# A state-space mixer and a gated MLP on one core: the first block's queues rearranged, and its first differences, clamps and skip moved between engines

## The chip, the cores and the metric

The kernel runs on one core of one Trainium2 chip. The metric is device time in microseconds (us), lower is better. The engines are PE (TensorE, the matrix engine), DVE (VectorE), ACT (ScalarE), POOL (GpSimd) and SP (SyncE, which issues the DMAs). Each works through its own queue in order and waits on semaphores for the others.

## The reference

Two sequences of 1024 tokens by 512 go through a mixer of the Mamba-2 kind and then a gated MLP, each behind a layer norm and with a residual. The change touches the mixer alone:

```python
x = x + mixer(layernorm(x)); x = x + ffn(layernorm(x))
proj = hidden @ W_in * mup_vector              # 512 -> 2368: z, xBC, dt
xBC  = silu(conv_b + sum(conv_w[:, k] * shift(xBC, k) for k in range(4)))
dt   = softplus(dt + dt_bias); dA = exp(-dt * exp(A_log))
state = state * dA + (dt * x)[..., None] * B   # 64 heads of 16, 128 states, one token after another
y = einsum(state, C) + D * x
g = y * silu(z); g = g * rsqrt(mean(g * g) + EPS) * norm_w
out = g @ W_out
```

## The kernel before, in words

The 1024 tokens are cut into 8 blocks of 128, and each block (both sequences side by side: 256 columns) into two steps of 64 tokens, numbered c = 0 to 15. Matmuls keep fp32 accuracy by splitting each operand into a rounded part (hi, made by ACT) and the rest (lo, made by DVE as raw minus hi), and by three products: hi hi, hi lo, lo hi (L1223 to L1225). The weights are split once, in the opening, in 14 pieces: `weight_hi(n)` on ACT (L624, L627) and `weight_lo(n)` on DVE (L880, L883). Pieces 0 to 9 are those of W_in and belong to the ten projections of a block, "project(j, e)"; pieces 10 to 13 are W_out. The raw pieces land in buffers that are used for something else later (the ring, xpad, sz, the state, rows, skip, sq, res), so whoever first writes such a buffer waits until that piece is split.

For each block: the rows are normalised (statistics on DVE, L890; the power on POOL, L509; L899), transposed by PE (L1209) and split (`norm_hi` L632, `norm_lo` L905). Projection 0 gives dt. ACT takes it out of PSUM in `evacuate(j, 0)` (four ACTIVATEs of L642, an exp behind a table load L646, a copy L649). DVE finishes softplus by a polynomial of 11 steps, `soft` (L911), and a running sum (L928). That sum goes out to DRAM and comes back broadcast in four 256 KB pieces, the ring. Projections 1 to 5 feed the convolution: ACT starts a pair of tiles (`first_taps`), DVE adds the other taps (`conv_taps`, L936, 30 instructions a block), ACT applies silu (L697). Projections 6 to 9 are z.

For each step, in four groups g of 16 heads: `diff` (POOL, L530) subtracts the ring from a token's own sum, `clamp` (ACT, L715) cuts it at zero, `fade` (ACT, L719) takes the exponential, `mix` (DVE, L991) multiplies it with the masked C B product (`mask_cb` L948), and PE multiplies with the inputs in `group(c, g)` (L1295). `make_xpad` (DVE, L977) prepares those inputs from the transposed x, `make_xw` (POOL, L539) the ones for the state, PE's `update(c, h)` (L1306) and DVE's `update_state` (L998 in step 0) carry the state on; `carry` (PE, L1272) reads it in the next step. Then `make_skip` (ACT, L725: D times x), `make_y` (L1006), `gate` (L1012), `gate_hi` (ACT, L732), `gate_lo` (L1017), and PE's projection out.

The order in which an engine does this is written by hand: each engine's part has a `body(i, first, last)` for a block, and a prologue before it for block 0. In `body` the projections of block i+1 stand between the groups of step 1 of block i. The prologue and the branches `if first` are run once.

## Time and profile before

| | us |
|---|---|
| median of 3 runs | 775.62 (775.45 to 776.03) |
| profiled execution, whole | 774.75 |
| its span | 773.0 |
| PE busy in the span | 742.7 (96%) |
| DVE busy | 518.6 (67%) |
| ACT busy | 492.7 (64%) |
| POOL busy | 294.0 (38%) |

The span runs from the first to the last instruction of the core; the whole execution is 1.75 us longer. Times in the rows are us from the span's start. A row of the timeline merges like instructions that stand behind one another (x and a count); "idle before" in brackets is the time in which the engine stood still, with the work that ended it. Busy time of PE says that an instruction was in flight, not that the array ran at its peak.

### The profile page before, as it was taken

How to read it: one execution, taken by the hardware profiler on the slowest of the kernel's cores; microseconds unless marked ns; L12 is line 12 of the kernel's file. 1: busy time of each engine (PE TensorE's matmuls, PEld its weight loads, DVE VectorE, ACT ScalarE, POOL GpSimd, SP SyncE). 2: the span in 40 equal slices, each digit the busy share in tenths (PEclk: the TensorE clock that was granted, in tenths of full speed). 3: DMA queues.
4: the chain of work that ended last, by engine and by line, in shares of the span. 5: the costliest groups of instructions: out<-in, count | busy, mean ns of one | idle time of the engine just before them, and what ended most of it. 6: DMA issues, size and time to landing. Idle time of an engine off the chain costs nothing.

```text
span 773.0 us, 20312 instructions
## 1 busy us (share of the span) xinstructions
PE 742.7 (96%) x8486; PEld 612.8 (79%) x8486; DVE 518.6 (67%) x845; ACT 492.7 (64%) x933; POOL 294.0 (38%) x235
## 2 busy tenths in 40 slices
PE   4887999999999999999999999889999999999998
PEld 4866888788887887887888887678888888888887
DVE  6968976886887797797797698763633532632331
ACT  6989978978978977978888888634312321321330
POOL 2173285366456536627708718540010011002002
PEclk9978999999999999999999999989999999999999
DMA  9823244484475266365376377855113003003002
GB/s 298 236 67 109 55 95 111 96 243 127 83 213 169 80 148 214 99 148 188 93 204 190 83 200 234 230 159 164 55 56 109 0 28 136 0 14 93 3 1 84
DMA packets 42300, 94.97 MB, mean 123 GB/s; under 512 B 9889, under 2 KB 15777, under 8 KB 42017
## 3 DMA queue, kind: packets, MB, share of 16 engines
q1 hardware_dynamic: 42208, 93.67, 42.6%
q8 instruction: 67, 1.10, 0.6%
q14 instruction: 25, 0.20, 0.1%
HBM read 84.73 MB, written 17.57 MB: 132 GB/s over the span
## 4 chain that ended last, share of the span: by engine, by line
PE 61%; DVE 21%; ACT 10%; issue 5%; DMA 2%; SPq 1%; POOL 1%; DVEq 0%; ACTq 0%; POOLq 0%
PE ps_y L1684 10%; PE ps_proj L1671 10%; DVE cx L936 9%; PE ps_out L1671 6%; PE ps_x L1671 6%; PE ps_proj L1223 4%; PE ps_proj L1224 3%; PE ps_proj L1225 3%; PE ps_x L1272 3%; PE ps_y L1295 3%; DVE ring L991 3%; ACT ring L715 2%; PE ps_out L1319 2%; DVE dt_p L911 2%; PE ps_out L1321 2%
## 5 line engine op out<-in xcount | busy, mean ns | idle before, releaser
L530 POOL TENSOR_TENSOR ring<-tokd,ring 128x1024 f32<-128x1024 f32 x64 | 122.5, 1927 | 189.4 <-ACT tokd L710 126.1
L1223 PE MATMUL ps_proj<-xn_hi,win_x_hi 128*128 128x256 f32 x352 | 104.7, 297 | 1.6 <-DVE xn_lo L905 1.6
L1224 PE MATMUL ps_proj<-xn_lo,win_x_hi 128*128 128x256 f32 x352 | 100.2, 285 | 0.0
L1225 PE MATMUL ps_proj<-xn_hi,win_x_lo 128*128 128x256 f32 x352 | 99.9, 284 | 0.0
L936 DVE SCALAR_TENSOR_TENSOR cx<-cin,consts,cx 128x256 f32<-128x256 f32 x240 | 96.4, 484 | 0.0
L1540 POOL TENSOR_TENSOR res<-res,hidden 128x512 f32<-128x512 f32 (+1 forms) x16 | 20.1, 1257 | 166.3 <-DVE hidden L1603 160.7
L1223 PEld LDWEIGHTS ps_proj<-xn_hi,win_x_hi 128*128 128x128 f32 x352 | 67.6, 192 | 14.8 <-issue 11.5
L991 DVE TENSOR_TENSOR ring<-ring,ps_tok 128x1024 f32<-128x1024 f32 x64 | 75.6, 1215 | 4.7 <-ACT ring L719 4.7
L1223 PE MATMUL ps_proj<-xn_hi,win_z_hi 128*128 128x256 f32 x256 | 74.4, 291 | 0.0
L715 ACT ACTIVATE ring<-ring 128x1024 f32<-128x1024 f32 x64 | 66.8, 1060 | 10.2 <-POOL ring L530 10.2
L1224 PE MATMUL ps_proj<-xn_lo,win_z_hi 128*128 128x256 f32 x256 | 72.5, 283 | 0.0
L1225 PE MATMUL ps_proj<-xn_hi,win_z_lo 128*128 128x256 f32 x256 | 72.4, 283 | 0.0
L1225 PEld LDWEIGHTS ps_proj<-xn_hi,win_x_lo 128*128 128x128 f32 x352 | 67.8, 193 | 0.0
L1224 PEld LDWEIGHTS ps_proj<-xn_lo,win_x_hi 128*128 128x128 f32 x352 | 67.8, 192 | 0.0
L719 ACT ACTIVATE ring<-ring 128x1024 f32<-128x1024 f32 x64 | 65.9, 1056 | 0.1
L1684 PE MATMUL ps_y<-wd,h_hi 128*128 128x512 f32 x165 | 65.8, 399 | 0.0
L1684 PE MATMUL ps_y<-wd,h_lo 128*128 128x512 f32 x165 | 65.0, 394 | 0.0
L1295 PEld LDWEIGHTS ps_y<-ring,xpad 64*32 64x32 f32 x4096 | 45.1, 107 | 20.2 <-issue 12.9
L1561 ACT ACTIVATE silu_g<-ps_out,scales 128x512 f32<-128x512 f32 x24 | 16.6, 691 | 68.0 <-PE ps_x L1671 68.0
L1295 PE MATMUL ps_y<-ring,xpad 64*32 64x64 f32 x4096 | 54.1, 228 | 3.6 <-DVE ring L991 3.0
L1563 ACT ACTIVATE h_hi<-hidden 128x512 fp32r<-128x512 f32 x44 | 27.9, 634 | 40.6 <-DVE hidden L1628 40.6
L548 POOL TENSOR_TENSOR state<-state,whole 128x2048 f32<-128x2048 f32 x14 | 53.1, 3790 | 0.0
(186 smaller groups left out, 1889.6 us busy)
## 6 DMA issues: line engine op xcount, KB each, us to landing
ring<-cum_dram SPq DMA_DIRECT2D x128, 256.0 KB, 5.0
xin<-x SPq DMA_DIRECT2D x8, 512.0 KB, 3.9
res<-x SPq DMA_DIRECT2D x32, 128.0 KB, 2.7
x_dram<-res SPq DMA_DIRECT2D x32, 128.0 KB, 3.1
res<-x_dram SPq DMA_DIRECT2D x16, 256.0 KB, 2.7
out<-res SPq DMA_DIRECT2D x15, 256.0 KB, 2.1
x_in_sb<-x_dram SPq DMA_DIRECT2D x3, 1024.0 KB, 5.6
gate_w_copy<-gate_w SPq DMA_DIRECT2D x4, 704.0 KB, 5.9
```

What stands on the lines that cost most here:

```text
L530: pool.tensor_tensor(ring[:, g, :, :], own, ring[:, g, :, :], ALU.subtract).then_inc(diffed, 1)
L548: pool.tensor_tensor(s, s, whole[:, :, j:j + 1].to_broadcast([P, BATCH * HEADS, HEAD]), ALU.mult).then_inc(state_faded, 1)
L715: act.activation(ring[:, g, :, :], ring[:, g, :, :], ACT.Relu).then_inc(clamped, 1)
L719: act.activation(ring[:, g, :, :], ring[:, g, :, :], ACT.Exp, scale=-1.0).then_inc(faded, 1)
L936: dve.scalar_tensor_tensor(cx[:, m, :, :], cin[:, m, :, k:k + Q], col(C_CW + 4 * m + k), cx[:, m, :, :], ALU.mult, ALU.add).then_inc(tap_m ...
L991: dve.tensor_tensor(ring[:, g, :, :], ring[:, g, :, :], ps_cb.unsqueeze(1).to_broadcast([P, GH, Q]), ALU.mult).then_inc(mixed, 1)
L1223: pe.matmul(out, hi[:, k, :], xn_hi[:, k, :], start=(k == 0), stop=False)
L1224: pe.matmul(out, hi[:, k, :], xn_lo[:, k, :], start=False, stop=False)
L1225: made = pe.matmul(out, lo[:, k, :], xn_hi[:, k, :], start=False, stop=(k == KT - 1))
L1295: made = pe.matmul(ps_y[32 * pair:32 * pair + 32, at:at + Q], xpad[half(b), g * GH + h, :], ring[half(b), g, h, :], start=(c == g == n == ...
L1671: made = pe.matmul(out_ps, a, b, start=(k == 0 and x is xn_hi), stop=(k == KT - 1 and x is xn_lo))
L1684: made = pe.matmul(ps_o[t % 2], a, b, start=(m == 0 and h is h_hi), stop=(m == MT - 1 and h is h_lo))
```

## The change

The changed parts all belong to the opening, that is the prologues and block 0; later blocks keep their order.

- The first rows are loaded, measured, scaled and normalised for each of the two sequences on its own. PE transposes an identity 20 times before the first rows and 6 times behind them (`keep_warm`).
- ACT's and DVE's prologues are reordered: `evacuate(0, 0)` stands between `weight_hi(2)` and `weight_hi(3)`, and three `soft` steps stand between `weight_lo(3)` and `weight_lo(4)`.
- In step 0 DVE does `diff` and `clamp` of the groups 0, 1 and 2 (`opening_diff`, `opening_clamp`); group 3 stays with POOL and ACT.
- In step 0 the skip product is one instruction of POOL, `pool_skip`, in place of eight on ACT.
- The pieces 9 to 13 are split later, and in other places; pieces of W_out land in another order of buffers.
- In block 0 PE does `update(0, 1)` and `group(0, 3)` before it transposes the next block's rows, and projection 9 before `turn_tokd`.

```diff
+        landing += [t[:].rearrange("p m t -> p (m t)") for t in (skip, sq)] + [rows[:], xres[:].rearrange("p m t -> p (m t)")]
...
 
         def piece(n):
...
-            sp.dma_start(xin[:], x_by_block[0]).then_inc(x_in, 16)
+            sp.dma_start(xin[:, 0, :], x_by_block[0, :, 0, :]).then_inc(x_first, 16)
+            sp.dma_start(xin[:, 1, :], x_by_block[0, :, 1, :]).then_inc(x_in, 16)
...
-            norm_scale(0)
+            def opening_scale(b):
+                pool.wait_ge(moments_made, b + 1)
+                pool.tensor_tensor(spread[:, b:b + 1], moments[:, b, 1:2], eps[:, b:b + 1], ALU.add).then_inc(eps_added, 1)
+                pool.wait_ge(eps_added, b + 1)
+                pool.tensor_tensor(rstd[:, b:b + 1], spread[:, b:b + 1], minus_half[:, b:b + 1], ALU.pow).then_inc(rstd_made, 1)
+
+            opening_scale(0)
+            opening_scale(1)
             pool.memset(chain[:, 0::Q], 0.0).then_inc(filled, 1)
-            pool.wait_ge(rstd_made, 1)
+            pool.wait_ge(xn_made, 2)
...
+            def pool_skip(c):
+
+                pool.wait_ge(y_made, c)
+                pool.wait_ge(conv_made, CT * (c // STEPS + 1))
+                at = BATCH * (c % STEPS)
+                pool.tensor_tensor(skip[:].rearrange("p m (b t) -> p m b t", b=BATCH), cx[:, 0:ZT, at:at + BATCH, :],
                                    consts[:, C_D:C_D + ZT].unsqueeze(2).unsqueeze(3).to_broadcast([P, ZT, BATCH, Q]),
                                    ALU.mult).then_inc(skip_made, 1)
...
+                    if opening:
+                        pool.wait_ge(diffed, GROUPS - 1)
+                        diff(0, 0, GROUPS - 1)
                     if not (opening or closing):
...
                     if closing:
-                        last_skip()
+                        pool_skip(c)
                     if not closing:
+                        if opening:
+                            pool.wait_ge(xn_made, 4)
                         for g in range(GROUPS):
+                            if opening and g == 1:
+                                pool.wait_ge(lo_made, LANDED_SKIP)
+                                pool_skip(c)
                             if g == GROUPS - 1 and not opening:
                                 rms_scale(c - 1, 1 - j)
                             diff(i + j, 1 - j, g)
...
             pool.wait_ge(filled, 4)
-            pool.wait_ge(tap_made, N_TAPS)
-            for g in range(GROUPS):
-                diff(0, 0, g)
             body(0, True, False)
...
                 c = STEPS * i
                 if not first:
                     evacuate(i, 6)
-                clamp(c, 0)
-                clamp(c, 1)
-                if not first:
+                if first:
+                    keep_tok(c)
+                    fade(c, 0)
+                else:
+                    clamp(c, 0)
+                    clamp(c, 1)
                     square(c - 1)
                     evacuate(i, 7)
-                keep_tok(c)
-                fade(c, 0)
-                clamp(c, 2)
+                    keep_tok(c)
+                    fade(c, 0)
+                    clamp(c, 2)
                 fade(c, 1)
+                if first:
+                    weight_hi(9)
+                    fade(c, 2)
+                    act.wait_ge(clamped, GROUPS - 1)
                 clamp(c, 3)
-                fade(c, 2)
+                if not first:
+                    fade(c, 2)
                 fade(c, 3)
-                if first:
-                    weight_hi(EVENTS)
-                else:
+                if not first:
                     make_skip(i, 0)
                 evacuate(i, 8)
-                keep_tokd(i, 1)
+                if not first:
+                    keep_tokd(i, 1)
                 evacuate(i, 9)
                 if first:
-                    weight_hi(EVENTS + 1)
+                    keep_tokd(i, 1)
+                    weight_hi(EVENTS)
                 if not last:
                     norm_hi(i + 1, 0)
                     norm_hi(i + 1, 1)
                 if first:
-                    for n in range(EVENTS + 2, PIECES):
-                        weight_hi(n)
-                    act.wait_ge(lo_made, LANDED_SKIP)
-                    make_skip(i, 0)
+                    weight_hi(EVENTS + 1)
...
                 clamp(c + 1, 0)
                 clamp(c + 1, 1)
+                if first:
+                    weight_hi(EVENTS + 2)
                 if not last:
                     evacuate(i + 1, 0)
                 gate_hi(c)
+                if first:
+                    weight_hi(EVENTS + 3)
...
             weight_hi(0)
-            weight_hi(1)
             norm_hi(0, 0)
             norm_hi(0, 1)
-            for n in range(2, 6):
-                weight_hi(n)
+            weight_hi(1)
+            weight_hi(2)
             act.wait_ge(zeroed, 7)
             evacuate(0, 0)
+            weight_hi(3)
             evacuate(0, 1)
+            weight_hi(4)
+            weight_hi(5)
+            evacuate(0, 2)
             first_taps(0, CONV_ORDER[0:2])
-            evacuate(0, 2)
+            evacuate(0, 3)
             first_taps(0, CONV_ORDER[2:4])
             weight_hi(6)
+            evacuate(0, 4)
+            first_taps(0, CONV_ORDER[4:6])
             make_run(0)
-            evacuate(0, 3)
-            first_taps(0, CONV_ORDER[4:6])
+            evacuate(0, 5)
+            first_taps(0, CONV_ORDER[6:8])
+            first_taps(0, CONV_ORDER[8:10])
             weight_hi(7)
-            evacuate(0, 4)
-            first_taps(0, CONV_ORDER[6:8])
-            evacuate(0, 5)
-            first_taps(0, CONV_ORDER[8:10])
             keep_tokd(0, 0)
...
-            weight_hi(9)
             body(0, True, False)
...
+            def opening_stats(b):
+                dve.wait_ge(x_in if b else x_first, 16)
+                dve.bn_stats(stats[:, b, :], xin[:, b, :]).then_inc(stats_made, 1)
+                dve.wait_ge(stats_made, b + 1)
+                dve.bn_aggr(moments[:, b, :], stats[:, b, :]).then_inc(moments_made, 1)
+
+            def opening_normalise(b):
+                dve.wait_ge(rstd_made, b + 1)
+                dve.tensor_scalar(xin[:, b, :], xin[:, b, :], moments[:, b, 0:1], rstd[:, b:b + 1],
+                                  ALU.subtract, ALU.mult).then_inc(xn_made, 1)
+
+            def opening_clamp(g):
+                dve.wait_ge(diffed, g + 1)
+                dve.tensor_scalar(ring[:, g, :, :], ring[:, g, :, :], 0.0, None, ALU.max).then_inc(clamped, 1)
+
+            def opening_diff(g):
+
+                dve.wait_ge(ring_in[g], 32)
+                dve.wait_ge(tokd_kept, 1)
+                own = tokd[:, 0, CUM, g * GH:(g + 1) * GH].unsqueeze(2).to_broadcast([P, GH, Q])
+                dve.tensor_tensor(ring[:, g, :, :], own, ring[:, g, :, :], ALU.subtract).then_inc(diffed, 1)
...
                 mask_cb(c)
                 make_xpad(i, 0)
-                if first:
-                    weight_lo(9)
-                else:
+                if not first:
                     make_x1(c - 2)
                 mix(c, 0)
                 if not first:
                     scale_carry(i, 0)
-                for g in range(1, GROUPS):
-                    mix(c, g)
-                if not last:
+                if first:
+                    opening_diff(2)
+                    opening_clamp(2)
+                mix(c, 1)
+                if first:
+                    weight_lo(9)
+                mix(c, 2)
+                if first:
+                    norm_stats(i + 1)
+                mix(c, 3)
+                if first:
+                    update_state(c, 0)
+                    normalise(i + 1)
+                    update_state(c, 1)
+                    weight_lo(EVENTS)
+                elif not last:
                     norm_stats(i + 1)
                     normalise(i + 1)
-                if first:
-                    weight_lo(EVENTS)
                 if last:
                     mlp_stats(0)
-                update_state(c, 0)
+                if not first:
+                    update_state(c, 0)
                 if last:
                     mlp_normalise(0)
                     mlp_normalise(1)
+                if not last:
+                    norm_lo(i + 1, 0)
+                    norm_lo(i + 1, 1)
                 if first:
                     weight_lo(EVENTS + 1)
-                if not last:
-                    norm_lo(i + 1, 0)
-                    norm_lo(i + 1, 1)
-                update_state(c, 1)
-                if first:
-                    for n in range(EVENTS + 2, PIECES):
-                        weight_lo(n)
+                else:
+                    update_state(c, 1)
                 make_y(c)
                 gate(i, 0)
+                if first:
+                    weight_lo(EVENTS + 2)
...
                 gate_lo(c - 1)
+                if first:
+                    weight_lo(EVENTS + 3)
                 for n in range(1, 4):
                     soft(i + 1, n)
...
-            norm_stats(0)
+            opening_stats(0)
+            opening_stats(1)
+            opening_normalise(0)
+            opening_normalise(1)
             weight_lo(0)
-            normalise(0)
-            weight_lo(1)
             norm_lo(0, 0)
             norm_lo(0, 1)
-            for n in range(2, 6):
+            for n in range(1, 4):
                 weight_lo(n)
-            for n in range(1, LOGN):
+            for n in range(1, 4):
+                soft(0, n)
+            weight_lo(4)
+            weight_lo(5)
+            for n in range(4, LOGN):
                 soft(0, n)
             make_dt(0, opening=True)
...
             conv_taps(0, CONV_ORDER[8:10])
+            opening_diff(0)
+            opening_clamp(0)
             weight_lo(8)
+            opening_diff(1)
+            opening_clamp(1)
             dve.wait_ge(zeroed, 8)
             body(0, True, False)
...
+            def keep_warm(n):
+
+
+                for _ in range(n):
+                    pe.transpose(ps_out[:, 0:P], eye[:], eye[:])
...
                 update(c, 0)
-                turn_tokd(i, 1)
                 if first:
                     pe.wait_ge(lo_made, EVENTS)
-                project(i, 9)
+                    project(i, 9)
+                    turn_tokd(i, 1)
+                else:
+                    turn_tokd(i, 1)
+                    project(i, 9)
                 group(c, 2)
+                if first:
+                    update(c, 1)
+                    group(c, 3)
                 if not last:
                     turn_xn(i + 1, 0)
                     turn_xn(i + 1, 1)
                 if not first:
                     sum_squares(c - 1)
-                update(c, 1)
-                group(c, 3)
+                    update(c, 1)
+                    group(c, 3)
...
             pe.wait_ge(filled, 1)
+            keep_warm(20)
             turn_xn(0, 0, True)
             turn_xn(0, 1, True)
+            keep_warm(6)
             for e in range(8):
                 pe.wait_ge(lo_made, e + 1)
                 project(0, e)
```

DVE, from the last taps of block 0's convolution to the last `mix` of step 0. Before (L936 taps, L880 `weight_lo`, L948 mask, L977 xpad, L991 mix):

```order
L936 SCALAR_TENSOR_TENSOR cx<-cin,consts,cx 128x256 x12
L880 TENSOR_TENSOR win_z_lo<-sz,win_z_hi 128x4x256
L948 TENSOR_TENSOR ps_tok<-ps_tok,causal 128x64
L977 TENSOR_TENSOR xpad<-ps_x,tokd 128x32x16 x2
L880 TENSOR_TENSOR win_z_lo<-state,win_z_hi 128x4x256
L991 TENSOR_TENSOR ring<-ring,ps_tok 128x1024 x4
```

and now (L985 taps, L943 `opening_diff`, L936 `opening_clamp`, L997 mask, L1026 xpad, L1042 mix):

```order
L985 SCALAR_TENSOR_TENSOR cx<-cin,consts,cx 128x256 x12
L943 TENSOR_TENSOR ring<-tokd,ring 128x1024
L936 TENSOR_SCALAR ring<-ring 128x1024
L907 TENSOR_TENSOR win_z_lo<-sz,win_z_hi 128x4x256
L943 TENSOR_TENSOR ring<-tokd,ring 128x1024
L936 TENSOR_SCALAR ring<-ring 128x1024
L997 TENSOR_TENSOR ps_tok<-ps_tok,causal 128x64
L1026 TENSOR_TENSOR xpad<-ps_x,tokd 128x32x16 x2
L1042 TENSOR_TENSOR ring<-ring,ps_tok 128x1024
L943 TENSOR_TENSOR ring<-tokd,ring 128x1024
L936 TENSOR_SCALAR ring<-ring 128x1024
L1042 TENSOR_TENSOR ring<-ring,ps_tok 128x1024
```

Three differences and three clamps have come in, `weight_lo(8)` stands behind the first pair and the mask behind the second.

POOL, from the zeroing of xpad on. Before (L530 diff, L539 xw, L507 and L509 the scale of the next rows, L556 the squares):

```order
L522 MEMSET xpad 128x2048
L530 TENSOR_TENSOR ring<-tokd,ring 128x1024 x4
L539 TENSOR_TENSOR xw<-xpad,tokd 128x1024
L507 TENSOR_TENSOR spread<-moments,eps 128x2
L509 TENSOR_TENSOR rstd<-spread,minus_half 128x2
L530 TENSOR_TENSOR ring<-tokd,ring 128x1024 x4
L556 TENSOR_TENSOR sq<-sq 128x512
L556 TENSOR_TENSOR sq<-sq 128x256
```

and now (L539 diff, L548 xw, L509 and L511 the scale, L586 the skip, L565 the squares):

```order
L531 MEMSET xpad 128x2048
L548 TENSOR_TENSOR xw<-xpad,tokd 128x1024
L539 TENSOR_TENSOR ring<-tokd,ring 128x1024
L509 TENSOR_TENSOR spread<-moments,eps 128x2
L511 TENSOR_TENSOR rstd<-spread,minus_half 128x2
L539 TENSOR_TENSOR ring<-tokd,ring 128x1024
L586 TENSOR_TENSOR skip<-cx,consts 128x1024
L539 TENSOR_TENSOR ring<-tokd,ring 128x1024 x3
L565 TENSOR_TENSOR sq<-sq 128x512
```

Step 0's diffs have shrunk to one behind xw, and the skip stands between step 1's first diff and its other three.

ACT, from the split of block 1's rows to the rounded gate of step 0. Before (L627 `weight_hi` of W_out, L725 skip, L715 clamps of step 1, L642 to L649 `evacuate(1, 0)`, L732 `gate_hi`):

```order
L632 ACTIVATE xn_hi<-ps_proj 128x4x128 x2
L627 ACTIVATE wout_hi<-sq,consts 128x512 x2
L627 ACTIVATE wout_hi<-res,consts 128x512 x2
L725 ACTIVATE skip<-cx,consts 128x128 x8
L715 ACTIVATE ring<-ring 128x1024 x2
L642 ACTIVATE dt_e<-ps_proj,consts 64x128 x2
L642 ACTIVATE dt_v<-ps_proj,consts 64x128 x2
L646 ACT_TABLE_LOAD
L646 ACTIVATE dt_e<-dt_e 128x128
L649 ACTIVATE dt_p<-dt_e 128x128
L732 ACTIVATE g_hi<-ps_y 128x1024
```

and now (L644 `weight_hi` of W_out, L732 clamps of step 1, L659 to L666 `evacuate(1, 0)`, L749 `gate_hi`):

```order
L649 ACTIVATE xn_hi<-ps_proj 128x4x128 x2
L644 ACTIVATE wout_hi<-sq,consts 128x512 x2
L732 ACTIVATE ring<-ring 128x1024 x2
L644 ACTIVATE wout_hi<-rows,consts 128x512 x2
L659 ACTIVATE dt_e<-ps_proj,consts 64x128 x2
L659 ACTIVATE dt_v<-ps_proj,consts 64x128 x2
L663 ACT_TABLE_LOAD
L663 ACTIVATE dt_e<-dt_e 128x128
L666 ACTIVATE dt_p<-dt_e 128x128
L749 ACTIVATE g_hi<-ps_y 128x1024
```

The eight skips are gone, and the clamps of step 1, the second of which needs POOL's second diff, now stand ahead of a piece's rounding.

## Rows read from the trace of the kernel before

**Rows 1.** Busy time per engine and stretch: stretch, its length, engines, granted PE clock, DMA.
```profile
12.00:14.00 2.00, 2.00 (x10) 2.00 (x10) 2.00 (x2) 1.61 (x2) 0.00 (x0) 1.00 1.10 348
...
18.00:20.00 2.00, 2.00 (x19) 2.00 (x18) 1.80 (x7) 1.87 (x5) 0.26 (x1) 1.00 1.08 368
...
40.00:50.00 10.00, 7.00 (x156) 6.44 (x156) 6.77 (x7) 9.97 (x12) 7.91 (x4) 0.67 0.03 10
70.00:80.00 10.00, 8.77 (x66) 7.09 (x64) 7.35 (x11) 9.77 (x15) 6.11 (x6) 1.00 0.23 71
130.00:220.00 90.00, 89.39 (x1375) 74.07 (x1375) 75.56 (x137) 76.71 (x159) 43.77 (x30) 1.00 0.53 132
```

**Rows 2.** PE's waits, 0 to 130 us: us in total, times, longest.
```profile
PE ps_proj L1209 <- POOL causal L516: 8.2, 1, 8.2
PE ps_y L1295 <- DVE ring L991: 3.0, 1, 3.0
PE ps_x L1306 <- DVE state L998: 2.9, 1, 2.9
...
PE ps_x L1272 <- DVE xpad L977: 1.9, 2, 1.2
```

**Rows 3.** Timeline of PE: start us, length us, line, operation, count, idle before.
```profile
11.73 0.55 PE L1223 MATMUL ps_proj<-xn_hi,win_x_hi 128*128 128x256 f32 x1 [1.60 <-DVE xn_lo L905]
...
29.83 0.39 PE L1223 MATMUL ps_proj<-xn_hi,win_z_hi 128*128 128x256 f32 x1
...
60.67 2.08 PE L1306 MATMUL ps_x<-xw,tok 64*128 64x512 f32 x4 [2.93 <-DVE state L998]
...
75.14 1.94 PE L1272 MATMUL ps_x<-state,cx 128*64 128x512 f32 x8 [1.23 <-DVE xpad L977]
...
85.28 1.13 PE L1306 MATMUL ps_x<-xw,tok 64*128 64x512 f32 x4
```

**Rows 4.** Timeline of DVE, 0 to 110 us, same columns.
```profile
14.02 2.37 DVE L880 TENSOR_TENSOR win_x_lo<-xpad,win_x_hi 128x1024 fp32r<-128x1024 f32 x2
17.61 3.56 DVE L911 SCALAR_TENSOR_TENSOR dt_p<-dt_p,dt_e 128x128 f32<-128x128 f32 x11 [1.22 <-ACT dt_p L649]
...
22.33 4.82 DVE L936 SCALAR_TENSOR_TENSOR cx<-cin,consts,cx 128x256 f32<-128x256 f32 x12
...
44.16 1.96 DVE L880 TENSOR_TENSOR win_z_lo<-state,win_z_hi 128x1024 fp32r<-128x1024 f32 x1
46.05 2.34 DVE L991 TENSOR_TENSOR ring<-ring,ps_tok 128x1024 f32<-128x1024 f32 x2
...
60.53 1.40 DVE L883 SCALAR_TENSOR_TENSOR wout_lo<-skip,consts,wout_hi 128x512 fp32r<-128x512 f32 x2
...
71.67 1.23 DVE L1017 TENSOR_TENSOR g_lo<-ps_y,g_hi 128x1024 fp32r<-128x1024 f32 x1 [2.35 <-ACT g_hi L732]
...
73.80 1.28 DVE L977 TENSOR_TENSOR xpad<-ps_x,tokd 128x512 f32<-128x512 f32 x2
```

**Rows 5.** Timeline of ACT, 0 to 110 us.
```profile
61.97 2.45 ACT L725 ACTIVATE skip<-cx,consts 128x128 f32<-128x128 f32 x8 [0.53 <-DVE wout_lo L883]
64.32 2.00 ACT L715 ACTIVATE ring<-ring 128x1024 f32<-128x1024 f32 x2
66.75 0.92 ACT L642 ACTIVATE dt_e<-ps_proj,consts 64x128 f32<-64x128 f32 x2 [0.43 <-PE ps_proj L1225]
...
68.64 1.28 ACT L646 ACT_TABLE_LOAD   x1
...
70.61 1.03 ACT L732 ACTIVATE g_hi<-ps_y 128x1024 fp32r<-128x1024 f32 x1
```

**Rows 6.** Timeline of POOL, 0 to 110 us.
```profile
36.70 8.34 POOL L530 TENSOR_TENSOR ring<-tokd,ring 128x1024 f32<-128x1024 f32 x4 [18.44 <-DVE cx L936]
45.01 2.91 POOL L539 TENSOR_TENSOR xw<-xpad,tokd 128x1024 f32<-128x1024 f32 x1
...
76.61 1.94 POOL L539 TENSOR_TENSOR xw<-xpad,tokd 128x1024 f32<-128x1024 f32 x1
```

16 lines of the change are left out of this document (8 added, 8 removed).

## The prediction

> **What bounds the kernel now.** I read the busy times by stretch first. From 130 to 220 us PE is busy for 89.39 of 90 us at the full granted clock, and DVE and ACT for about 76 each [rows 1]. So a later block gives nothing back and swallows nothing: whatever time PE is ahead or behind when block 0 is done arrives at the end. The change touches only block 0 and the prologue, so the whole question is when PE gets through them.
>
> PE's waits come next. Four stretches in the opening sum to 16.0 us: 8.2 for the first normalised rows, 3.0 for the first `mix`, 2.9 for the copied state, 1.9 for xpad [rows 2]. The clock adds to them. PE does 10 projection matmuls in 2 us at 12 to 14 us and 19 at 18 to 20 us [rows 1]: the first is the pace of 1.2 GHz, the second that of 2.4 GHz, although the granted-clock column reads 1.00 in both, so at the very start the pace is to be believed and not the column. Around the wait of 3.0 us that column itself falls, to 0.67 over 40 to 50 us [rows 1].
>
> Last I read the timelines of DVE, ACT and POOL for what those waits hang on, and laid both kernels' queues out on paper: each instruction starts when the one before it on its engine and its semaphores are done, with the lengths of the rows. The same sheet for the old order agrees with its trace to 0.3 us up to 57 us and runs 1.7 to 2 us late from 60 us on; I come back to that.
>
> **The change, part by part.**
>
> *Rows by batch, warm-up.* The scale of one sequence overlaps the statistics of the other, and ACT and DVE no longer round weight piece 1 between rows and PE. The first projection starts at 9.65 instead of 11.73 us [rows 3] and, if 26 transposes have raised the clock, its 12 matmuls take 1.3 us and not 2.4. PE would finish projection 5 at 25.4; it used to go on to projection 6 at 29.83, behind a short transpose of 0.8 [rows 3]: 3.6 us ahead. The transposes themselves cost nothing, PE was idle for 8.2 us there [rows 2].
>
> *That lead is lost at once.* Projection 6 needs `weight_lo(6)`, and that stands on DVE behind everything before it. ACT now does `evacuate(0, 0)` before `weight_hi(3)`, so DVE gets piece 3 only at 14.95 us and stands idle for 2.8 us. The old queue idled 1.22 us there [rows 4]. From 14.95 DVE has no gap: three pieces at 1.18 (3.5), 11 soft steps at 0.32 (3.6), dt and the sum 1.16, twelve taps 4.8: 28.0, then piece 6 until 29.1 us (2.37 for two pieces, 3.56 for 11 steps, 4.82 for 12 taps [rows 4]). PE waits there from 26.5 on. The old kernel had piece 6 at 22.33 + 4.8 + 1.2 = 28.3 [rows 4] and started that projection at 29.83 [rows 3]. So 0.7 us of 3.6 are left, and the taps end 0.7 us later, at 37.2.
>
> *Differences and clamps on DVE.* POOL needed 8.34 us for four differences [rows 6]. DVE now takes three, with three clamps. A difference has two SBUF inputs like `weight_lo`: 1.18 us [rows 4]. A clamp on DVE is nowhere in the trace. ACT's takes 1.0 [rows 5]; below, it can't cost less than one soft step of an eighth of the elements, 0.32; above, not more than a two-input instruction, 1.2. I take 1.0. Behind the taps DVE does 2 x (1.2 + 1.0) and one piece, until 42.7; then mask and xpad, until 44.1: no later than before, since the mask used to wait for ACT. The first `mix` starts at 44.1 instead of 46.05 [rows 4], a gain of 1.9. But the third difference now meets POOL's xw. Beside POOL one `weight_lo` took 1.96 instead of 1.18 us [rows 4] and xw 2.91 instead of 1.94 [rows 6]: the excess of each is the rest of the other's instruction. So `opening_diff(2)` waits until 46.2, and the second `mix` ends at 49.5 instead of 46.05 + 2.34 = 48.4 [rows 4]: PE's first update is a us late.
>
> The Trainium skill, "SBUF — State Buffer", section "SBUF: two separate sides", says that this pair of ports is locked for the whole instruction and that an instruction of DVE with two SBUF inputs blocks against POOL. By that rule, the trace agrees with its 1.96 and 2.91 us, and it speaks against this change, which gives DVE three more such instructions while POOL works; without it the sum below would be a us smaller. The Trainium skill, "VectorE: DVE Perf Modes", section "The perf-mode tier table", says that an fp32 `tensor_scalar` between SBUF operands runs at twice the rate of a `tensor_tensor`; by that a clamp would be an estimated 0.65 us and the sum 0.9 less. No row here shows it.
>
> *PE in step 0.* Projection 9 ends near 55.7 on the sheet, old and new, but now `update(0, 1)` and `group(0, 3)` follow at once and the state is copied before the normalisation: `group(0, 3)` is done at 58.9; it used to follow an update that ended at 62.75 [rows 3], so at 63.9. The next rows are turned behind that and no more ahead of it, but their DVE half comes at 62.0 and not at 60.53 + 1.40 + 1.2 = 63.1 [rows 4], and projection 0 of block 1 ends at 63.9 and not at 66.75, where ACT had waited for it [rows 5]. Here the change is 2.8 us ahead.
>
> *The skip, and what stands behind it.* ACT is rid of 2.45 us [rows 5]. But the skip's buffer is free only after `weight_lo(10)`, which now follows `update_state(0, 1)`: 60.8 us. POOL's skip is the size of xw, 1.94 us [rows 6]: no row shows it, the bounds are a difference beside nothing (8.34 / 4 = 2.09 with one blocked) and xw blocked (2.91). It ends at 62.9. Only then does `diff(1, 1)` start; it shares the ports with piece 11 and ends at 65.45. ACT's queue waits for it: `clamp(1, 1)` is now ahead of piece 12, of `evacuate(1, 0)` and of `gate_hi`. From there: clamp 1.0 [rows 5], piece 12 1.25 (DVE's like piece takes 1.40 [rows 4]), four ACTIVATEs 1.87, table, exp and copy from 68.64 to 70.61, 1.97 [rows 5]: `gate_hi` starts at 71.5 against 70.61, 0.9 late. DVE had already waited 2.35 us for it [rows 4]; from `gate_lo` to xpad it took 73.80 - 71.67 = 2.13, and now piece 13 stands between (1.4, as the two instructions at 60.53 [rows 4]). So xpad of step 1 starts at 73.80 + 0.9 + 1.4 = 76.1.
>
> *The clock.* PE ends projection 2 of block 1 some 1.4 us earlier than before, near 72.5, and then waits about 5 us for that xpad; it used to wait 1.23 [rows 3], which left the clock at 1.00 [rows 1]. Four matmul records of an update took 2.08 us at the half clock and 1.13 at the full [rows 3]; a carry of 1.94 [rows 3] would take 3.6, so 1.6 lost, and a projection 24 x (0.2 - 0.105) = 2.3. What DVE does behind it hides part. I take 1.0, with bounds 0 and 3.8.
>
> **Sum.** 0.9 + 1.4 + 1.0 = 3.3 us later. My sheet is that late for the old kernel because it lets POOL's difference go before the second half of a piece, which the trace did the other way round; the like place here, `diff(1, 1)` and piece 11, is worth 0.65, and I take off 0.5. **2.8 us slower.** Against its own execution: span 773.0 + 2.8 = 775.8, whole 774.75 + 2.8 = 777.55. The median of the runs is 0.87 above that execution, hence 778.4.
>
> **The rivals.**
>
> *A, the lead arrives (faster).* If POOL gets to `diff(1, 1)` by 62 us, ACT starts `evacuate(1, 0)` when projection 0 of block 1 ends (64.0): + 1.87 + 1.97 = `gate_hi` at 67.8, xpad at 67.8 + 1.06 + 2.13 + 1.4 = 72.4, 1.4 earlier than before; with block 1's projections 2.8 ahead, up to 2.8. For it: PE really is ahead at 63.9, and the skip has left ACT. Against it: piece 10 would have to be split by 58 us, and three differences, three clamps and the state stand before it. Time 775.6 - 2.1 = 773.5.
>
> *B, no change.* Clamps at 0.65 (-0.9), the ports taken in the better order and the clock kept (-1.0): 0.9 is left, 776.5. For it: each of the three is open. Against: all must come together.
>
> *C, the clock stays down (clearly slower).* Carry and projection both run at half: 3.8 instead of 1.0, so 781.2. It decides from an idle of about 3 us, the length that was followed by half clock [rows 1, 2]. Against it: DVE's chain behind xpad, as full as PE's, hides some.
>
> *D, the warm-up warms nothing.* Then the first projection's end, `evacuate(0, 0)`, piece 3 and the whole of DVE's queue come 1.1 us later; 779.5. It lies within my forecast's range.
>
> **How the numbers follow.** Forecast with D: 0.50, its own range 777.2 to 780.2. C: 0.12. B, of which most lies within 0.2%: 0.13. A: 0.25. About 0.2% (1.55 us) is what a measurement of this kernel can tell from no change. The forecast and C are slower (0.62). The range runs from A's middle less a little, 773.0, to C, 781.2.
>
> **What would show it.** In the changed profile: the first projection before 10 us at the quick pace; a wait of PE of 2 us or more near 27 to 29 us, ended by `weight_lo(6)`; the first `mix` near 44 us with `opening_diff(2)` stretched beside xw; POOL's skip near 61 us; ACT idle before `clamp(1, 1)`; PE idle for 4 to 5 us before the carry, xpad at 76, and a granted clock below 1.00 in 75 to 82. I am wrong if DVE stands at `weight_lo(10)` before 58 us, or if xpad starts before 74.

## The result, and the profile after

The changed kernel takes 783.62 us, median of 4 runs (781.83 to 786.68). The kernel before took 775.83 us beside it (4 runs), and the ratio is 1.009, 95% interval 1.0066 to 1.0114. In a second comparison, on another chip, it took 784.85 against 776.7 us, ratio 1.0106 (1.0081 to 1.013). So it is slower by 7.8 to 8.2 us. The forecast was 778.4 with a range of 773.0 to 781.2: the sign was right and the size too small by 5 us.

The opening first. The same stretches as in [rows 1], after the change:

```profile
12.00:14.00 2.00, 2.00 (x20) 2.00 (x19) 0.84 (x1) 1.91 (x6) 0.00 (x0) 1.00 1.10 348
...
40.00:50.00 10.00, 5.47 (x154) 4.80 (x156) 9.93 (x11) 5.01 (x6) 4.34 (x2) 0.96 0.22 63
70.00:80.00 10.00, 5.25 (x23) 2.29 (x22) 5.98 (x11) 9.94 (x17) 4.41 (x5) 0.83 0.35 105
130.00:220.00 90.00, 89.34 (x1374) 73.95 (x1372) 73.58 (x133) 77.91 (x162) 45.00 (x33) 1.00 0.52 128
```

In the first row PE does 20 records in 2 us and not 10: the warm-up works. In 40 to 50 us DVE is full and ACT half idle. In 70 to 80 us PE is busy for 5.25 us, not 8.77, at a granted clock of 0.83. A later block looks as before. PE's waits up to 100 us, against [rows 2]:

```profile
PE ps_x L1351 <- DVE xpad L1026: 4.7, 1, 4.7
PE ps_y L1374 <- DVE ring L1042: 4.2, 2, 3.0
PE ps_proj L1302 <- DVE win_z_lo L907: 3.6, 2, 2.2
```

Now the timelines, up to 76 us. Lines have moved with the change: L936 is `opening_clamp`, L943 `opening_diff`, L907 and L910 are `weight_lo`, L1026 is `make_xpad`, L749 `gate_hi`, L732 `clamp`, L539 POOL's `diff`, L1321 `turn_tokd`, L1374 `group`, L1398 to L1400 the output projection (L1321 in the kernel before). DVE, against [rows 4]:

```profile
38.41 0.69 DVE L936 TENSOR_SCALAR ring<-ring 128x1024 f32<-128x1024 f32 x1
...
43.35 1.21 DVE L1042 TENSOR_TENSOR ring<-ring,ps_tok 128x1024 f32<-128x1024 f32 x1
44.47 2.10 DVE L943 TENSOR_TENSOR ring<-tokd,ring 128x1024 f32<-128x1024 f32 x1
...
61.20 3.68 DVE L910 SCALAR_TENSOR_TENSOR wout_lo<-sq,consts,wout_hi 128x512 fp32r<-128x512 f32 x2
...
71.47 1.23 DVE L1069 TENSOR_TENSOR g_lo<-ps_y,g_hi 128x1024 fp32r<-128x1024 f32 x1 [1.74 <-ACT g_hi L749]
72.68 1.42 DVE L910 SCALAR_TENSOR_TENSOR wout_lo<-res,consts,wout_hi 128x512 fp32r<-128x512 f32 x2
...
75.00 1.28 DVE L1026 TENSOR_TENSOR xpad<-ps_x,tokd 128x512 f32<-128x512 f32 x2
```

ACT, against [rows 5], and POOL, against [rows 6]:

```profile
64.37 1.06 ACT L732 ACTIVATE ring<-ring 128x1024 f32<-128x1024 f32 x1 [2.25 <-POOL ring L539]
...
70.41 1.03 ACT L749 ACTIVATE g_hi<-ps_y 128x1024 fp32r<-128x1024 f32 x1
```

```profile
60.13 1.90 POOL L586 TENSOR_TENSOR skip<-cx,consts 128x1024 f32<-128x1024 f32 x1 [1.91 <-DVE wout_lo L910]
61.99 6.53 POOL L539 TENSOR_TENSOR ring<-tokd,ring 128x1024 f32<-128x1024 f32 x3
```

PE, against [rows 3], and then two places far behind the changed code:

```profile
9.31 0.36 PE L1302 MATMUL ps_proj<-xn_hi,win_x_hi 128*128 128x256 f32 x1 [0.85 <-DVE xn_lo L954]
...
76.33 3.52 PE L1351 MATMUL ps_x<-state,cx 128*64 128x512 f32 x8 [4.75 <-DVE xpad L1026]
...
219.45 0.56 PE L1321 MATMUL ps_tok<-eye,dts 64*64 64x64 f32 x10
222.75 0.44 PE L1321 MATMUL ps_tok<-eye,dts 64*64 64x64 f32 x6 [2.74 <-issue]
...
511.02 2.73 PE L1374 MATMUL ps_y<-ring,xpad 64*32 64x64 f32 x235
517.76 0.64 PE L1374 MATMUL ps_y<-ring,xpad 64*32 64x64 f32 x21 [4.01 <-issue]
```

The last two bracketed idle times are the surprise. PE stops in the middle of `turn_tokd`, after 10 of 16 equal matmuls, and in the middle of a `group`. "issue" means that nothing the profile shows held it. The same work in successive steps, first start after minus first start before (us), tells where the time went:

| mark | before | after minus before |
|---|---|---|
| xpad, step 1 of block 0 | 73.80 | +1.20 |
| xpad, step 0 of block 1 | 108.07 | +2.26 |
| xpad, step 1 of block 2 | 194.68 | +2.47 |
| `carry`, step 1 of block 3 | 258.06 | +6.33 |
| `carry`, step 1 of block 6 | 440.87 | +7.06 |
| `make_x1`, last but one | 516.03 | +11.33 |

The opening costs 2.3 us. The stall near 222 us costs 3.9 and not only its 2.74: the matmuls behind it start 0.43 us apart and not 0.23 until 226.5 us, and the granted clock was 0.50 over 224 to 226. The stall near 518 costs 4.3 more, beyond what the kernel before loses there itself (it has a stall of 1.95 us at 509.80, shown below); here too the granted clock was 0.50, over 519 to 522. The profiled executions are 786.68 and 774.75 us; that is further apart than the medians.

### The profile page after: what moved, and what is told of

Same layout as the page of the kernel before. It is cut to its first block, busy times and chain, and to the rows that moved or that the text cites. A ratio compares the mean times of both kernels' runs of the same rounds, so it can differ in the third digit from the quotient of the medians.

```text
span 784.9 us, 20361 instructions
## 1 busy us (share of the span) xinstructions
PE 748.2 (95%) x8512; PEld 616.4 (79%) x8512; DVE 524.2 (67%) x851; ACT 487.3 (62%) x922; POOL 290.0 (37%) x235
## 4 chain that ended last, share of the span: by engine, by line
PE 59%; DVE 23%; ACT 7%; issue 6%; DMA 2%; POOL 1%; SPq 1%; DVEq 0%; POOLq 0%; ACTq 0%
DVE cx L985 10%; PE ps_y L1771 10%; PE ps_proj L1758 9%; PE ps_out L1758 6%; PE ps_x L1758 6%; PE ps_proj L1302 3%; PE ps_x L1351 3%; PE ps_y L1374 3%; PE ps_proj L1303 3%; PE ps_proj L1304 3%; DVE ring L1042 3%; DVE dt_p L960 2%; PE ps_out L1398 2%; PE ps_out L1399 2%; PE ps_out L1400 2%
## 5 line engine op out<-in xcount | busy, mean ns | idle before, releaser
L539 POOL TENSOR_TENSOR ring<-tokd,ring 128x1024 f32<-128x1024 f32 x61 | 116.9, 1929 | 167.9 <-ACT tokd L727 129.7
L985 DVE SCALAR_TENSOR_TENSOR cx<-cin,consts,cx 128x256 f32<-128x256 f32 x240 | 96.3, 476 | 0.0
L1042 DVE TENSOR_TENSOR ring<-ring,ps_tok 128x1024 f32<-128x1024 f32 x64 | 75.6, 1213 | 3.6 <-ACT ring L736 3.6
L732 ACT ACTIVATE ring<-ring 128x1024 f32<-128x1024 f32 x61 | 63.8, 1059 | 12.9 <-POOL ring L539 12.8
L736 ACT ACTIVATE ring<-ring 128x1024 f32<-128x1024 f32 x64 | 66.0, 1056 | 4.3 <-DVE ring L936 4.2
L1374 PEld LDWEIGHTS ps_y<-ring,xpad 64*32 64x32 f32 x4096 | 44.5, 105 | 24.1 <-issue 15.5
L1374 PE MATMUL ps_y<-ring,xpad 64*32 64x64 f32 x4096 | 53.6, 225 | 8.2 <-DVE ring L1042 4.2
L1302 PEld LDWEIGHTS ps_proj<-xn_hi,win_z_hi 128*128 128x128 f32 x256 | 49.2, 192 | 6.3 <-DVE win_z_lo L907 4.0
L1398 PE MATMUL ps_out<-wout_hi,g_hi 128*128 128x512 f32 x120 | 52.0, 433 | 1.9 <-DVE res L1078 1.9
```

The costliest lines, as they stand in the source:

```text
L539: pool.tensor_tensor(ring[:, g, :, :], own, ring[:, g, :, :], ALU.subtract).then_inc(diffed, 1)
L732: act.activation(ring[:, g, :, :], ring[:, g, :, :], ACT.Relu).then_inc(clamped, 1)
L736: act.activation(ring[:, g, :, :], ring[:, g, :, :], ACT.Exp, scale=-1.0).then_inc(faded, 1)
L985: dve.scalar_tensor_tensor(cx[:, m, :, :], cin[:, m, :, k:k + Q], col(C_CW + 4 * m + k), cx[:, m, :, :], ALU.mult, ALU.add).then_inc(tap_m ...
L1042: dve.tensor_tensor(ring[:, g, :, :], ring[:, g, :, :], ps_cb.unsqueeze(1).to_broadcast([P, GH, Q]), ALU.mult).then_inc(mixed, 1)
L1302: pe.matmul(out, hi[:, k, :], xn_hi[:, k, :], start=(k == 0), stop=False)
```

## The experiments

The theory under test: PE's program comes in by DMA in blocks of 256 entries, and when PE reaches the border of a block before the next one has arrived, it stands still, and the profile says "issue". (The recorded expectations call such a block "a piece of 16384 bytes" or "a fetched piece"; it has nothing to do with the 14 pieces of weights.) An edit that adds entries early on moves every later border to another instruction. The rivals are that the stalls follow the later traffic, or that they are chance. An edit to PE's queue that does no work can tell them apart.

Each was timed against the kernel before on its own chip. "Slots" are the queue entries that PE has more than in the kernel before: a transpose is a weight load and a matmul, 2 slots; a plain fp32 matmul turned out to be 4. The numbers are counted from the edits. In the traces all kernels that begin with transposes or plain matmuls have one record less than that (51, 127, 255 and so on), because one wait has gone from ahead of the first rows; pad52, pad256 and after_cold have theirs exactly. Line numbers move by a few from kernel to kernel with such an edit.

| kernel | slots | median, us | before, us | ratio (95%) | stalls by "issue" over 1 us behind 85 us |
|---|---|---|---|---|---|
| before_again | 0 | 777.03 | 776.70 | 1.0012 (0.9991 to 1.0034) | 2.63 |
| pad52 | 52 | 782.86 | 777.32 | 1.0071 (1.0046 to 1.0096) | 3.07, 4.31 |
| before128 | 128 | 784.56 | 777.16 | 1.0106 (1.007 to 1.0142) | 3.03, 3.58 |
| pad256 | 256 | 799.40 | 777.32 | 1.0288 (1.027 to 1.0306) | 3.41 |
| before_warm256 | 256 | 776.34 | 776.70 | 0.9995 (0.9978 to 1.0013) | 3.72 |
| after_again | 52 | 784.85 | 776.70 | 1.0106 (1.0081 to 1.013) | 2.92, 4.16 |
| lo13_late | 52 | 785.05 | 777.32 | 1.0089 (1.0068 to 1.011) | 1.26, 3.13, 4.08 |
| after_cold | 0 | 780.13 | 777.32 | 1.0044 (1.0024 to 1.0064) | 2.10, 1.37 |
| after_hot | 88 | 778.83 | 776.49 | 1.0023 (1.0004 to 1.0042) | 3.93 |
| after_fill | 460 | 786.00 | 776.49 | 1.0117 (1.0079 to 1.0155) | 2.56, 4.33 |
| after_piece | 256 | 777.84 | 777.16 | 1.0002 (0.9981 to 1.0023) | 1.22, 1.81 |
| best256 | 460 | 785.56 | 776.49 | 1.0118 (1.0083 to 1.0154) | 2.56, 2.63 |
| best152 | 252 | 776.38 | 776.49 | 1.0002 (0.9982 to 1.0022) | 2.89 |
| bestwarm128 | 128 | 780.31 | 777.16 | 1.0048 (1.0026 to 1.007) | 2.38, 3.33 |
| bestwarm256 | 256 | 774.65 | 777.16 | 0.9965 (0.9946 to 0.9983) | 2.79 |

**The kernel before with 52 slots more.** The waits are satisfied already, and PE is idle there. Two waits share a slot: the trace has 52 records more for the 104 waits.

```diff
             pe.wait_ge(filled, 1)
+            for _ in range(104):
+                pe.wait_ge(filled, 1)
```

> The kernel before, with 52 satisfied semaphore waits more at the head of PE's queue, where PE stands idle until 8.2 us anyway: as many queue slots as the 26 transposes (26 weight loads and 26 matmuls) of the changed kernel, and no other change. Theory (PE's program is fetched in 16384-byte pieces, and where a border of a piece falls decides whether PE runs dry): the stalls of PE that no engine releases move or grow, the opening stays as before to 0.2 us, and the time rises by 1 to 6 us, to 777 to 782. Rival (the stalls come from the traffic that is 2.5 us later, or are chance): within 1 us of before, 775 to 777.

PE's timeline of this kernel, whose work is that of the kernel before, line for line:

```profile
217.87 0.50 PE L1242 MATMUL ps_tok<-eye,dts 64*64 64x64 f32 x9
221.44 0.69 PE L1242 MATMUL ps_tok<-eye,dts 64*64 64x64 f32 x7 [3.07 <-issue]
...
518.77 0.64 PE L1295 MATMUL ps_y<-ring,xpad 64*32 64x64 f32 x22 [4.31 <-issue]
```

These are the two stalls of the changed kernel, in the same `turn_tokd` and the same `group`, one matmul away, as the one record between 51 and 52 has it. The kernel before had, in its whole trace, one such stall of over a us, in the output projection of the last block:

```profile
509.80 0.50 PE L1321 MATMUL ps_out<-wout_hi,g_lo 128*128 128x512 f32 x1 [1.95 <-issue]
```

So 52 entries that do nothing bring both late losses, and 5.5 of the 8 us. Of these 1.0 is in the opening of its profile, which was not expected (0.2 at most): the granted clock over 62 to 68 us was 0.50 and not 0.60.

**A whole block more.** The same edit with 512 waits, 256 slots.

> The kernel before with 256 such waits, which is one whole piece of 16384 bytes at 64 bytes each: the borders fall where they fell before. Theory: time of before to 1 us (plus what 256 waits cost beyond the 8.2 us in which PE is idle; the start of the first projection at 11.73 shows that). Rival (any shift costs): slower by as much as with 52 or more.

```profile
30.05 1.94 PE L1209 MATMUL ps_proj<-eye,xin 128*128 128x128 f32 x8 [30.05 <-issue]
...
534.13 0.50 PE L1321 MATMUL ps_out<-wout_hi,g_lo 128*128 128x512 f32 x1 [3.41 <-issue]
```

The waits cost more than the idle time that was to hide them: the first transposes start at 30.05 and not at 8.19, 21.9 us later. That explains 799.40 - 777.32 = 22.1 us but for 0.2, as the theory asked; the rival asked for at least the loss of pad52 on top. The stall is back at the line of the kernel before, and none stands in the `turn_tokd` that had one with 52.

**The changed kernel without its warm-up, and with piece 13 behind xpad.**

```diff
-            keep_warm(20)
...
-            keep_warm(6)
```

> The changed kernel without its 26 transposes. The 0.5 us that the first projections gain by a warm array are lost, at most 1.5. Theory: the instruction borders go back to about those of before, the stall of 2.74 us at 222.75 goes or moves, and the time falls from 783.6 to 778 to 781. Rival (the transposes have no part in the late stalls): 783 to 785.

```diff
-                if first:
-                    weight_lo(EVENTS + 3)
...
                 make_xpad(i, 1)
+                if first:
+                    weight_lo(EVENTS + 3)
```

> The changed kernel with the split of the last piece of W_out (1.42 us on DVE at 72.68) moved behind the second x-pad, all else as in it. Expected: x-pad of step 1 at 73.6 in place of 75.0, the carry begins 1.4 earlier, and PE's idle time before it falls from 4.7 to 3.3 us. If the clock still falls, the gain is 1.4 us; if it holds, 1.4 + 1.6 = 3.0 us. The stalls of PE in later blocks stay, since PE's queue is the same: 780.6 to 782.3. Rival (the 5 us outside the changed code follow the opening's lateness): over 3 us are gained, 780 or less.

Without the transposes block 1 comes 5.03 us late (the mark that is +2.26 above): in the new order the warm-up is worth 2.8 us, far over the 1.5 expected. Still the kernel as a whole lies 2.8 us over the kernel before and not 8: the stalls at 222 and 518 us are gone, and the two that it has (511.94 and 516.07 us) sum to 3.5 us and not to 6.8. With piece 13 late, xpad of step 1 stands at -0.23 in place of +1.20, as expected. The clock fell all the same, behind 3.34 us of idle time, only later: the granted clock was 0.50 from 76.3 to 79.7 us, so the carry took 2.39 us and the projection behind it lost the rest. Block 1 is 1.34 late and not 2.26, so 0.9 of the 1.43 is kept. The time misses the 780.6 to 782.3 that was expected, and no gain can be made out (785.05 against 777.32, as the changed kernel's 784.85 against 776.70). Its profile has one more stall of over a us, 1.26 at 181 us, at the border where the changed kernel has one of 0.42.

**A wrong count that told something.** `fill` issues plain fp32 matmuls:

```diff
+            def fill(n):
+                for _ in range(n):
+                    pe.matmul(ps_out[0:32, 0:8], eye[0:32, 0:32], eye[0:32, 0:8], start=True, stop=True)
...
+                if e == 6:
+                    fill(51)
                 pe.wait_ge(lo_made, e + 1)
...
+            fill(51)
             pe.wait_ge(zeroed, 8)
```

> The changed kernel with 102 tiny matmuls more on PE (32 rows, 8 columns, 51 of them where PE waits for projection 6 and 51 where it waits before block 0): with the 26 transposes that makes 256 queue slots more than before, one whole piece of 16384 bytes. Theory (borders of the fetched pieces): the stalls of 2.7 us near 222 and of 4.0 near 518 go, only one of about 2 to 3.4 us near 512 stays, as in the kernel before; the opening stays 2.3 late: before plus 2 to 3.5 us, 777 to 779.5 where before is 775.5. Rival (more instructions are more stalls, or chance): 783 or more, as the changed kernel.

The expectation failed, and by my own count: the trace has 204 weight loads and 204 matmuls of that line for 102 calls. The shift was 460 slots, that is 204 past a whole block, and the stalls stood at a third pair of places (103.88 and 521.24 us). Nor were the second 51 calls free: xpad of step 1 is 3.80 late here and 1.20 in the changed kernel. Repeated with 51 calls, all ahead of projection 6:

> The changed kernel with 51 tiny fp32 matmuls more where PE waits for projection 6. Each is run as two weight loads and two matmuls, so with the 26 transposes PE's queue is 52 + 204 = 256 slots longer than before: one whole piece. Theory (borders of the fetched pieces): no stall of 2.7 near 222 us, none in group 3 near 518; one of 2 to 3.4 us at L1321's counterpart in the first output projection of the last block, near 512, as in the kernel before; marks of block 1 2.3 to 3 us late and still 2.3 to 3.5 late at 475. Time: before plus 2 to 3.5 us (778.5 to 780 where before is 776.5), against plus 8 for the changed kernel. Rival: plus 7 or more, with the stalls where they were.

Here the borders are those of the kernel before but for one record, all else is the changed kernel, and the time is level with before: over 7 us of the 8 are gone. That is more than the theory asked. Its 2 to 3.5 us were for the opening, and block 1 is still 2.00 late in the profile, but the ratio of 1.0002 (0.9981 to 1.0023) leaves no room for them. The stall in the output projection is back, with a smaller one, 1.22 at 509.59 us, one border ahead of it:

```profile
513.71 0.39 PE L1404 MATMUL ps_out<-wout_hi,g_lo 128*128 128x512 f32 x1 [1.81 <-issue]
```

**The carry's clock.** 18 transposes more (`if first: keep_warm(18)` ahead of `carry(i, 1)`) in the idle time.

> The changed kernel with 18 transposes of the identity more, in the 4.7 us in which PE waits for the x-pad of step 1 (71.6 to 76.3). Theory of the clock: the carry behind them runs at full clock and takes 1.94 in place of 3.52 us, so that all marks of block 1 come 1.6 us earlier (2.26 late becomes 0.7 late). Rival (the carry is slow for another cause, the transfers of the ring): the marks stay 2.3 late. The 36 queue slots more move the borders of the fetched pieces to a place that was not seen yet, so the whole time can go either way by 4 us: 777 to 785.

```profile
71.42 2.13 PE L1281 MATMUL ps_out<-eye 128*128 128x128 f32 x18
76.36 3.60 PE L1351 MATMUL ps_x<-state,cx 128*64 128x512 f32 x8 [2.81 <-DVE xpad L1026]
```

The clock fell all the same, with 2.81 us of idle time left: the marks stay 2.37 late. So by this run alone the rival stood. The total is 2.3 us over before, as much as the opening costs: at 88 slots one stall is left.

**Three edits together.** ACT evacuates ahead of the clamp that waits for POOL, piece 13 is late as above, and `fill` sets the borders.

```diff
                 clamp(c + 1, 0)
-                clamp(c + 1, 1)
                 if first:
                     weight_hi(EVENTS + 2)
-                if not last:
+                    evacuate(i + 1, 0)
+                clamp(c + 1, 1)
+                if not (first or last):
                     evacuate(i + 1, 0)
```

> The changed kernel with three edits: ACT's evacuation of the next block's dt stands ahead of the clamp of group 1 (which waited 2.25 us for POOL), the last piece of W_out is split behind the x-pad of step 1, and the 102 tiny matmuls of the fill make the shift one whole piece. Expected by the theory: gate_hi at 68.1 in place of 70.4, x-pad of step 1 at 71.3 in place of 75.0, PE idle 1 us before the carry, clock held, marks of block 1 about 2.4 earlier than in the kernel before; late stalls as before. Time: before minus 1.5 to 3 us, 772.5 to 774 where before is 775.5. Rival (borders have no part): 5 us above that.

> As the one with 102 tiny matmuls and the reordered ACT and DVE, but with 50 of them, so that PE's queue is 152 slots longer than before and the borders fall elsewhere. Same opening. Theory: the stalls that no engine releases stand at other places than with 52 or 256 slots and have another sum, between 0.5 and 9 us: 771 to 780. Rival (borders have no part): the time of the one with 102, within 1 us, and stalls at the same places.

Both counts are wrong in the same way: 460 and 252 slots, so neither expectation was tested as it was meant. The first, expected at 772.5 to 774, took 785.56. It has the large stalls of after_fill, in the same places of the program, 4 to 9 us earlier in time. The second, 4 slots short of a whole block, takes 9 us less. Not all of that is the borders: the second 51 calls of `fill`, which it lacks, cost 1.8 us at xpad of step 1. Its one stall of over a us, 2.89 at 505.75, stands in a `group`, one border ahead of that of the kernel before. Its marks are 2.05 early at xpad of step 1, and 0.97 in block 1: `gate_hi` at 68.0 did what was expected, the carry at half clock took a us back:

```profile
73.08 3.52 PE L1356 MATMUL ps_x<-state,cx 128*64 128x512 f32 x8 [3.00 <-DVE xpad L1027]
```

Then 24 transposes were put into those 3.0 us, with 39 or 7 calls of `fill`:

> The changed kernel with the ACT evacuation ahead of the waiting clamp, the last piece of W_out behind the x-pad, 24 transposes in the 3.0 us in which PE waits for that x-pad, and 39 tiny matmuls, 256 slots in all. With 50 tiny matmuls and without the 24 transposes the marks of block 1 were 0.97 us earlier than in the kernel before, and the carry took 3.52 us. Theory of the clock (it fell because PE stood idle for 3 us): the carry takes 1.9 us and the marks are 2.3 to 2.6 us earlier than before. Rival (the clock falls all the same): 1.0 earlier, or a little less. Late stalls as in the kernel before. Time: before minus 1.5 to 2.5 us by the theory, within 1 us of before by the rival.

> The same with 7 tiny matmuls in place of 39: 128 slots more than before in all, half a piece. Opening as in the other. Theory of the borders: stalls elsewhere than with 256; their sum between 0.5 and 8 us, and at the same places of the program as in the kernel before with 128 slots more, whatever the time at which these are reached.

PE's timeline and the stretches 72 to 76 us with 256 slots:

```profile
71.76 2.78 PE L1282 MATMUL ps_out<-eye 128*128 128x128 f32 x24
74.47 1.94 PE L1356 MATMUL ps_x<-state,cx 128*64 128x512 f32 x8
```

```profile
72.00:74.00 2.00, 2.00 (x21) 2.00 (x20) 2.00 (x5) 2.00 (x4) 1.20 (x1) 1.00 0.00 0
74.00:76.00 2.00, 2.00 (x13) 0.78 (x11) 2.00 (x3) 2.00 (x5) 1.84 (x3) 1.00 0.00 0
```

And the same stretches without the 24 transposes, in best152:

```profile
72.00:74.00 2.00, 0.92 (x4) 0.37 (x6) 2.00 (x3) 2.00 (x5) 1.55 (x2) 0.82 0.00 0
74.00:76.00 2.00, 2.00 (x8) 0.31 (x4) 2.00 (x3) 2.00 (x4) 1.92 (x3) 0.50 0.00 0
```

With no idle time left the carry runs at full clock, 1.94 us: the theory of the clock holds, and the 18 transposes had been too few. Its rival, the transfers of the ring, falls too: in best152 the granted clock was 0.50 while the DMA engines moved nothing (the last two columns). The marks gained less than expected (0.6 and not 2.3 early), since here the transposes themselves stood in front of the carry: xpad began at 72.11, the carry at 74.47. This version is the only one faster than before: 0.9965. Why it is, is not shown. Its block 1 comes 0.57 us early, that of best152 0.97 early, and best152 is level with before.

**128 slots in both orders.**

```diff
             pe.wait_ge(filled, 1)
+            fill(32)
```

> The kernel before with 32 tiny matmuls (128 slots) at the head of PE's queue, where PE is idle until 8.2 us. Opening as before to 1 us (these matmuls may keep the array warm for a moment). Theory of the borders: stalls at the same places of the program as in the reordered kernel with 128 slots more, another sum than with 0 or 52: before minus 2 to plus 6. Rival (chance, or only the number of instructions): stalls as before.

PE's timeline, first the order of before, then the reordered kernel with as many slots:

```profile
160.12 0.79 PE L1246 MATMUL ps_tok<-eye,dts 64*64 64x64 f32 x9 [3.03 <-issue]
...
516.95 0.94 PE L1299 MATMUL ps_y<-ring,xpad 64*32 64x64 f32 x59 [3.58 <-issue]
```

```profile
158.44 0.50 PE L1326 MATMUL ps_tok<-eye,dts 64*64 64x64 f32 x9 [2.38 <-issue]
...
512.43 1.13 PE L1379 MATMUL ps_y<-ring,xpad 64*32 64x64 f32 x59 [3.33 <-issue]
```

The same two places to the matmul (9 and 59 left to do), reached 1.7 and 4.5 us apart. The time of the first, 7.4 us over before, lies outside the expected minus 2 to plus 6: the places were forecast, their price was not.

**Both kernels again, and the warm-up alone.** The last one, before_warm256, is the kernel before with `keep_warm(20)` and `keep_warm(6)` where the change has them, and 25 and 26 calls of `fill` in PE's idle time.

> The kernel before once more, unchanged. Theory (the first profile, 774.75 us, was an early execution): marks of block 1 up to 1 us later than in it, the stall at L1321 in the last block between 2 and 3.5 us at the same place, no stall of over 1 us near 222 or in group 3 near 518. Time within 1 us of the kernel before. Rival: the same marks to 0.2 us, and then the opening of the changed kernel costs 2.3 us in full.

> The changed kernel once more, unchanged. Theory: stalls at L1321 (dts) near 222 and at group 3 of the last block near 518 again, 2.5 to 4.5 us each, sum 6 to 8 us; the carry of step 1 at half clock, 3.5 us. Time: before plus 6 to 8.5 us. Rival (the stalls of the first profile were chance): other places.

> The kernel before with the 26 warm-up transposes alone, and 51 tiny matmuls in PE's idle time so that the queue is 256 slots longer, a whole piece. Without them the changed kernel's block 1 came 2.8 us later, so the warm-up is worth up to 2.8 us there; in the order of before projection 1 waits for its split weights, so less can be left. Theory: marks of block 1 0.5 to 2 us earlier than before, stalls as before: before minus 0.5 to 2.5 us. Rival (the warm-up only counts in the changed order): within 0.5 us of before.

The second profile of the changed kernel has its stalls at the same two instructions (2.92 and 4.16 us) and a slow carry, 3.40 us. That of the kernel before has 2.63 at L1321, and marks 0.57 us earlier than the first profile, not later: my idea of an early first execution fell. The warm-up alone gives 0.3 us over that at block 1, and a ratio of 0.9995 and not the 0.5 to 2.5 us that were expected: its rival holds, the warm-up only counts in the changed order.

**The count that settles it.** I counted PE's records (weight loads, matmuls, waits and some 40 register operations) ahead of every stall by "issue" over 0.35 us behind 85 us, in the 17 profiles. There are 42, and each count leaves 193 when divided by 256. With every such idle time of over 0.15 us there are 60, and it is 193 in all 60. Some of them:

```
kernel          records ahead of each stall        mod 256
before          3521, 14785                        193, 193
pad52           5825, 11969, 14785                 193, 193, 193
before128       4033, 10177, 12993, 14785          all 193
after           4545, 5825, 14785                  all 193
after_fill      2497, 14529, 15041                 all 193
bestwarm256     15041                              193
```

The remaining 63 entries of the first 256 I take to be some that the profile does not record; that is not shown. The DMA view has transfers of instructions, of 16384 bytes each, 67 in the run; with 256 entries in each that makes 17152, and PE has 17187 records in the kernel before. Over 218 to 224 us of the changed kernel (packets, MB, share of 16 engines):

```profile
q1 hardware_dynamic: 430, 1.41, 101.8%
q8 instruction: 1, 0.02, 1.3%
```

The one transfer of instructions (q8) begins at 219.84 us and takes 1.27 us, while the ring's transfers fill the DMA engines. PE reaches the border at 220.01 and goes on at 222.75, 2.9 us after the transfer's start. In the first profiles of both kernels no border up to 620 us is passed sooner than 2.2 us after its transfer began. What differs is when the transfer starts. Counted in PE's entries, it began between 44 ahead of the border before and 222 behind it. At the two stalls of the changed kernel it began when all 256 were done, at the stall of the kernel before with 255. So these stalls are transfers that started too late for the pace at which PE ran through its block. Near 518 us that was 256 entries in 1.6 us.

The Trainium skill, "Runtime: NRT & Kernel Launch", section "Instruction fetch mechanics", says that an engine's program is refilled in blocks of 256 instructions while the current one runs, and that crossing a block is mostly hidden. The first half agrees with the count of 193 and the 16384 bytes; "mostly" holds for all but one to five of some 60 borders in each trace (stalls of over 0.35 us), and these cost up to 4.3 us each.

## Why the prediction was wrong in size

The sum was 0.9 + 1.4 + 1.0 - 0.5 = 2.8 us. As measured at xpad of step 1 and at block 1 it was -0.2 + 1.4 + 1.06 = 2.26 us. The mechanism of the opening was right, its path and its size; what failed is what the sum left out. Term by term:

- **The opening as a whole: +2.26 us at block 1, in both profiles.** Right, to half a us. It is 2.26 against the first profile of the kernel before; against its second, 2.83.
- **First projection** 9.31 (9.65 predicted), at the quick pace. Right. **Projection 6** waits 2.16 us for `weight_lo(6)`, from 26.87 to 29.03. Right; the old place, 29.83, was nearly lost again.
- **A clamp on DVE** took 0.69 us, not the 1.0 I took, within my bounds. That is why the first `mix` stood at 43.35 and not at 44.1. `opening_diff(2)` beside xw took 2.10, as priced. (The Trainium skill, "VectorE: DVE Perf Modes", section "The perf-mode tier table", gave the estimate of 0.65 for the clamp; the trace agrees.)
- **PE in step 0.** The update that was to be a us late was not: the second `mix` ended at 48.4 and not at 49.5. Projection 0 of block 1 ended at 63.0 and not at 63.9 (before: 66.75), and nothing of that lead arrived.
- **`gate_hi`** stood at 70.41, not 71.5: 0.2 early and not 0.9 late. The chain was the one named (piece 10, POOL's skip at 60.13, `diff(1, 1)`, ACT idle 2.25 us before its clamp), but ran 0.7 to 1.1 us earlier; piece 11 in turn was stretched to 3.68. `diff(1, 1)` began at 61.99, just inside the 62 us that rival A asked for, and A did not come: ACT still stood before the clamp until 64.37, and `evacuate(1, 0)` began at 66.56 and not at 64.0. best152 shows what it was worth: with the evacuation ahead of that clamp `gate_hi` came 2.4 earlier.
- **Piece 13 ahead of xpad** cost 1.4: lo13_late gave back 1.43 there. With -0.2 for `gate_hi` that puts xpad at 75.00 and not at 76.1.
- **The clock** cost 1.6 in the carry (3.52 and not 1.94), of which 1.06 reached block 1; I took 1.0. bestwarm256 shows the cause. The granted clock was 1.00 again from 80 us on, right behind the carry, so rival C did not come as it was described.
- **The term that was missing** is 5 to 6 us. The step of the prediction that failed is its first: "a later block gives nothing back and swallows nothing". It rested on how full PE is [rows 1], which says nothing of whether PE's own instructions arrive. A stall of 1.95 us by "issue" at 509.80 stood in the trace of before, unread. And "the transposes themselves cost nothing, PE was idle" was true of their time and false of their 52 places in the queue: after_piece takes that shift away and the loss with it; pad52 adds it to the kernel before and has 5.5 us of it. In its place the runs show stalls at the block borders, 2.74 and 4.01 us long against 1.95 before, each with a stretch at half clock behind it: +3.9 and +4.3 us in the table of marks.

What stays open. The two measures of the shift don't agree: 5.5 us by pad52, all of the 8 by after_piece, which is level with before in the times though its block 1 is 2.0 us late in its profile. So the 2.3 us of the opening are shown in the profiles, and not in the median times. after_cold is like it: 5.0 late at block 1, and 2.8 in the time. Both profiled executions of the kernel before (774.75 and 772.06) lie below the medians of its other runs (775.6 to 777.3), so the average execution of it loses 1 to 5 us that I have not seen. And what held the late transfers of instructions back was not settled: near 222 us the DMA engines were full (101.8%), near 518 only half (0.50 over 513 to 517.7 us).

## What to carry to other kernels

Where an engine's program is thousands of entries long and its work comes in bursts of short instructions, any edit that changes the number of its entries early on moves every later refill; test a change together with a shift of the borders before you judge it (here 52 entries cost 5.5 us, and 256 in before_warm256 none). Read the idle times that "issue" ends, in the kernel before too, and count the entries ahead of them. A lead on the way to a wait is worth only what the last of its queues lets through.

## What the hardware showed that I had not expected

- PE's stalls by "issue" stand at one remainder of the entry count, 193 of 256, in 42 of 42 cases, with 0.38 to 4.33 us each.
- Satisfied waits are no filler: 256 slots of them, begun when the identity was ready at 2.10 us, ended at 30.05, 0.11 us each.
- A plain fp32 matmul of 32 x 8 appears as two loads and two matmuls; 50 such calls took 3.55 us.
- The carry met half clock, all or in part, with 4.75, 3.34, 3.00 and 2.81 us of idle time ahead of it (3.38 to 3.68, 2.39, 3.52 or 2.95, and 3.60 us long), and not with 2.00, 1.23 or none (1.94 us).
